# Attention scores by pairs of heads, a PSUM bank for each head, a list prefill in 22 pieces, and idle products in the front

## What is computed

```python
def attn(xn, in_proj_weight, out_proj_weight):        # xn [16, 256, 128]
    q, k, v = split_heads(xn @ in_proj_weight.T)      # 16 heads of 8
    attention = q @ k.T / sqrt(8) + causal_mask
    x = softmax(attention) @ v
    return x @ out_proj_weight.T

def ffn(xn, ...):                                     # inner width 352
    out = expert(xn, sg, su, sd)                      # the shared expert
    w = top2_of_softmax(xn @ wr.T + rb)               # 7 routed experts
    for e in range(7):
        out = out + w[..., e:e + 1] * expert(xn, rg[e], ru[e], rd[e])
    return out

x = x + attn(xn, ...) + ffn(xn, ...)
```

## Time and profile before

| | us |
|---|---|
| median of 3 runs | 547.07 |
| range of the runs | 542.17 to 549.5 |
| the profiled execution | 548.51 |
| its span | 546.8 |
| mean granted TensorE clock | 0.92 of full speed |

### The profile page before, as it was taken

The page is one execution under the profiler, slowest core; times in us unless marked ns, Lnnn a source line. Parts: engine busy times, 40 slices in busy tenths (PEclk is TensorE's granted clock), DMA queues, the critical chain, the costliest instruction groups (busy, mean ns, idle before and its releaser), DMA issues.

```text
span 546.8 us, 11856 instructions
## 1 busy us (share of the span) xinstructions
PE 487.8 (89%) x3924; PEld 355.8 (65%) x3924; DVE 388.4 (71%) x916; ACT 305.5 (56%) x543; POOL 309.8 (57%) x402
## 2 busy tenths in 40 slices
PE   2689987788899898898888779999999999999996
PEld 2667654455566565555555448888888888888884
DVE  5683688589978786777776227777777777776885
ACT  2434444446556566565555536666666666566654
POOL 1324466467763778788788700555555555584462
PEclk9875579779979999999999659999999999999999
DMA  8461478997765545554534253766666666502262
GB/s 259 144 187 48 112 288 306 366 309 248 253 207 184 157 143 150 162 164 151 167 102 152 63 218 107 247 225 233 216 227 213 238 233 241 201 17 79 91 202 93
DMA packets 53308, 101.18 MB, mean 185 GB/s; under 512 B 10295, under 2 KB 27584, under 8 KB 49280
## 3 DMA queue, kind: packets, MB, share of 16 engines
q1 hardware_dynamic: 48384, 91.95, 51.1%
q0 software_dynamic: 4864, 8.48, 4.7%
HBM read 60.91 MB, written 41.05 MB: 186 GB/s over the span
## 4 chain that ended last, share of the span: by engine, by line
PE 59%; issue 3%; ACT 2%; DVE 2%; POOL 1%; DVEq 0%; POOLq 0%; ACTq 0%
PE ps L624 12%; PE ps L625 12%; PE ps L626 11%; PE ps L754 4%; PE ps L684 3%; PE ps L678 2%; PE ps L863 2%; PE ps L764 2%; PE ps L690 2%; PE ps L852 2%; PE ps L744 2%; PE ps L757 1%; PE ps L700 1%; PE ps L766 1%; ACT sb_work L519 1%
## 5 line engine op out<-in xcount | busy, mean ns | idle before, releaser
L478 POOL DMA_INDIRECT ys<-sb_v_all,sb_xn_all x88 | 88.2, 1002 | 91.1 <-DVE sb_v_all L1135 66.4
L519 ACT ACTIVATE sb_work<-ps 128x1536 f32<-128x1536 f32 x64 | 92.9, 1452 | 45.2 <-PE ps L684 45.2
L443 POOL TENSOR_SCALAR_AFFINE_SELECT sb_work<-sb_work 128x768 f32<-128x768 f32 (+1 forms) x128 | 78.5, 639 | 65.4 <-DVE sb_mexp L1031 11.6
L1016 DVE TENSOR_REDUCE sb_negm<-ps 128x4 f32<-128x1024 f32 x64 | 78.3, 1223 | 46.5 <-PE ps L696 43.7
L624 PE MATMUL ps<-sb_ring,sb_wb 128*128 128x512 f32 x222 | 92.2, 415 | 2.3 <-DVE sb_ring L1109 1.6
L625 PE MATMUL ps<-sb_ring,sb_wb 128*128 128x512 f32 x222 | 88.7, 400 | 0.0
L626 PE MATMUL ps<-sb_ring,sb_wb 128*128 128x512 f32 x222 | 88.0, 396 | 0.0
L1123 DVE TENSOR_TENSOR sb_ring<-sb_work,sb_ring 128x512 fp32r<-128x512 f32 x90 | 64.4, 716 | 27.6 <-ACT sb_ring L587 21.8
L587 ACT ACTIVATE sb_ring<-sb_work 128x512 fp32r<-128x512 f32 x90 | 56.9, 632 | 46.2 <-DVE sb_work L1117 38.3
L1117 DVE TENSOR_TENSOR sb_work<-ps,sb_work 128x512 f32<-128x512 f32 x90 | 62.0, 689 | 24.7 <-ACT sb_work L581 16.4
L581 ACT ACTIVATE sb_work<-ps 128x512 f32<-128x512 f32 x90 | 53.7, 596 | 34.8 <-PE ps L626 26.2
(11 more groups left out here) (150 smaller groups left out, 1011.0 us busy)
## 6 DMA issues: line engine op xcount, KB each, us to landing
sb_wb<-wd SPq DMA_DIRECT2D x23, 1152.0 KB
sb_ring<-qk SPq DMA_DIRECT2D x64, 256.0 KB
wd<-sb_wb SPq DMA_DIRECT2D x8, 1152.0 KB, 6.1
sb_xn_all<-xs SPq DMA_DIRECT2D x22, 260.0 KB
qk<-sb_qk_h SPq DMA_DIRECT2D x16, 256.0 KB
qk<-sb_qk_l SPq DMA_DIRECT2D x32, 128.0 KB
qk<-sb_qk_h SPq DMA_DIRECT2D x32, 128.0 KB
sb_v_all<-ys SPq DMA_DIRECT2D x16, 256.0 KB, 3.1
```

What stands on the lines that cost most here:

```text
L443: pool.affine_select(out=o, in_=o, compare_op=ALU.is_ge, fill=0.0, base=0, pattern=[[0, o.shape[1]], [1, 128]], channel_multiplier=-1)\
L478: pool.indirect_dma_start(out=ys_d, out_offset=bass.IndirectOffsetOnAxis(ap=row, axis=0), in_=yst[i % NYS][:, EMB * j:EMB * j + EMB], in_o ...
L519: act.activation(P[n % 2], TR, ACT.Exp, scale=SCALE).then_inc(s["ex"], 1)
L1016: dve.tensor_reduce(negm[:, 1, :], SR[:, 256:1280].rearrange("p (h k) -> p h k", h=4), AX.X, ALU.max, negate=True).then_inc(s["maxa"], 1)
```

## The change

S and T get a bank for each head: S of head h in bank h, T of heads 0 and 2 in bank 4 and of 1 and 3 in bank 5, 384 columns each. The heads are served as two pairs. `scores(n, half)` forms S of one pair and T of the other, so each group of eight products meets four banks. Behind the first half come the transposes of quad n - 2 and the sums of quad n - 1, then the second half, then a wait for the normalization, the side products and the fold. `R1` is gone. The maxima come in two halves of two reductions each; between them stands the normalization, behind them the low part, `mexp` (now three buffers) and the routing piece. The exponential and the select come in two halves too, and the select waits for its exponential alone. The semaphore counts follow. The first two folds move from the front to its end. The prefill goes out in 22 pieces, one in each of the steps -1 to 20. TensorE gets 40 products of 512 columns whose result nobody reads: 22 at the start, 8 before the first v projection, 2 in each of the first five rounds of the front. In the front VectorE normalizes the first four token tiles ahead of the split of the small weights, and side results of steps below -4 go to banks 0 to 3.

```diff
-S0_AT, S1_AT = (0, 128, 1280, 1408), (256, 512, 768, 1024)
-T0_AT, T1_AT = (0, 512, 768, 1024), (256, 384, 1408, 1280)
+HEAD = 384
+PAIRS = ((0, 1), (2, 3))
...
+        S = [ps[:, h, 0:HEAD] for h in range(4)]
+        T = [ps[:, 4 + h % 2, 0:HEAD] for h in range(4)]
...
-            return J[:, 256:512] if n < -4 and n % 4 == 1 else X[:, 256:512]
+            return ps[:, n % 4, 256:512] if n < -4 else X[:, 256:512]
...
-                if n in (3, 5, 7, 9):
-                    if n == 3:
+                if 0 <= n + 1 < NR:
+                    if n == -1:
                         sp.wait_ge(s["ones1"], 1)
-                    a, z = [NR * k // 4 for k in ((n - 3) // 2, (n - 1) // 2)]
-                    sp.dma_start(xs_d.rearrange("(p a r) e -> p a (r e)", p=128, r=SUB)[:, a:z, :],
-                                 ones.unsqueeze(1).to_broadcast([128, z - a, SUB * ROW])).then_inc(s_zero, 16)
+                    rows = xs_d[TS * (n + 1):TS * (n + 2), :].rearrange("(p j) e -> p (j e)", j=SUB)
+                    sp.dma_start(rows, ones).then_inc(s_zero, 16)
...
-                    if isq(n + 3):
-                        pool.wait_ge(s["mx"], n + 4)
-                    if n < len(ROUTING):
-                        pool.wait_ge(s["rt"], sum(ROUTING[:n + 1]))
-                    pool.wait_ge(s["ex"], n + 1)
-                    for o in (parts[:, 0:12:2, :], parts[:, 3:12:8, :]):
+                    for k, pair in enumerate(PAIRS[::-1]):
+                        pool.wait_ge(s["ex"], 2 * n + k + 1)
+                        o = P[n % 2][:, HEAD * pair[0]:HEAD * pair[0] + 512].rearrange("p (k q) -> p k q", q=128)
                         pool.affine_select(out=o, in_=o, compare_op=ALU.is_ge, fill=0.0, base=0,
...
-                    act.wait_ge(s["ST"], n + 1)
-                    act.activation(P[n % 2], TR, ACT.Exp, scale=SCALE).then_inc(s["ex"], 1)
+                    for k, pair in enumerate(PAIRS[::-1]):
+                        act.wait_ge(s["ST"], 2 * n + k + 1)
+                        part = P[n % 2][:, HEAD * pair[0]:HEAD * pair[0] + 2 * HEAD]
+                        act.activation(part.rearrange("p (k h q) -> p h k q", h=2, q=128),
+                                       ps[:, 4:6, 0:HEAD].rearrange("p h (k q) -> p h k q", q=128), ACT.Exp,
+                                       scale=SCALE).then_inc(s["ex"], 1)
...
+            def scores(n, half):
                 m = n + 3
+                (a, b), (c, d) = PAIRS[half], PAIRS[1 - half]
                 if isq(m):
                     pe.wait_ge(s_qk[m % NK], m // NK * 16 + 16)
                     if m:
-                        pe.wait_ge(s["maxa"], m)
-                        pe.wait_ge(s["maxb"], m)
+                        pe.wait_ge(s["max"], 2 * m - 1 + half)
                 if isq(n):
                     pe.wait_ge(s["q4b"], n + 1)
-                    if n:
-                        pe.wait_ge(s["ex"], n)
+                    if n or half:
+                        pe.wait_ge(s["ex"], 2 * n + half)
...
-                pe.wait_ge(s["R1"], n + 4)
...
             def step(n):
                 b, j = quad(n)
                 if isq(n) or isq(n + 3):
-                    scores(n)
-                if n > -4:
-                    bank_read(n - 1)
-                side(n)
+                    scores(n, 0)
                 if isq(n - 2):
+                    bank_read(n - 1)
                     pe.wait_ge(s["OT"], n - 1)
                     for t in range(2):
                         last = pe.transpose(X[:, 128 * t:128 * t + 128], ot[:, 128 * t:128 * t + 128], ident)
                     last.then_inc(s["T"], 1)
                 if isq(n - 1):
+                    sums(n - 1)
+                if isq(n) or isq(n + 3):
+                    scores(n, 1)
+                if n > -4:
+                    bank_read(n - 1)
+                if isq(n - 2):
+                    pe.wait_ge(s["nm"], n - 1)
+                side(n)
+                if n >= 0 and isq(n + 2):
+                    maxima(n + 2)
...
+            def idle(count):
+                for _ in range(count):
+                    pe.matmul(X[:, :], busy[:, 0:128], busy[:, :], start=True, stop=True, skip_group_check=True)
+            pe.wait_ge(s["busy"], 1)
+            idle(22)
...
+                def maximum(half):
+                    a, b = PAIRS[half]
+                    dve.wait_ge(s["S"], 2 * m + half + 1)
+                    if half == 0 and m:
+                        dve.wait_ge(s["mx"], m)
+                    dve.tensor_reduce(negm[:, 1, a:b + 1], ps[:, a:b + 1, 0:256], AX.X, ALU.max, negate=True)
+                    dve.tensor_reduce(negm[:, 0, a:b + 1], ps[:, a:b + 1, 256:HEAD], AX.X, ALU.max, negate=True)\
+                        .then_inc(s["max"], 1)
```

233 lines of the change are left out of this document (109 added, 124 removed).

## The result

The changed kernel takes 546.9 us (median of 20 runs, 543.1 to 551.6), the kernel before 543.8 beside it (20 runs, 540.4 to 549.5). The ratio is 1.0056, with a 95% interval of 1.0029 to 1.0083: slower by half a per cent, where the prediction had it 0.7% faster. The profiled execution of the changed kernel took 551.6 us (span 549.9), in a slow state that 2 of its 20 runs show; that of before took 548.5.

The account below looks back on a forecast made before the run. Bound before: a ring of scores, all maxima, scores again, with GpSimd and VectorE close behind. Steps 5 to 22 -2, five routing steps +1, 32 late steps -3.5, rest 0: total -4, 542.3 to 543 us; range 525 to 560.

Parts of the forecast that it names:

- the one on GpSimd's waits: GpSimd's selects, freed from waits, may collide with VectorE's mexp and routing operations: 0.1 us a step, bounds 0 and 0.45.
- the slow rival: Collisions on VectorE cost 0.45 us per routing step (+8), four more low-clock spells +8: 559 us; chance 0.23.
- The rule that was weighed: GpSimd and VectorE share one port pair; by the rule, routing products collide as the cast does, giving the slow rival's time.
- the neutral case: Whole kernel: gain and loss cancel, likeliest at chance 0.42, its own range 536 to 552 us.
- VectorE and the normalization: TensorE waits for the normalization, late by VectorE's list of 3.65 us: routing steps 4.0 us, 0.25 slower than 3.76.
- GpSimd late: Steps 27 to 61: GpSimd's work with sends is a floor of 3.57 us a step; 3.65 taken, against 3.76 before.
- The ring: Old attention step: scores, all maxima, scores again; step = offset of the second score group + 2.6 us.
- ScalarE: One exponential becomes two of 0.81 us, +0.17 a step, hidden; 0.3 us lost in one step of four.
- Prefill: 22 small pieces instead of four remove the long q and k load stall: 3 us of DMA stalls left of 6.4.
- Idle products: 40 unread TensorE products cost some time and might keep the clock high: 0 taken for the sum.
- Low clock: After stalls, two spells at 1.2 GHz of about 2 us each; one should go with its stall.
- no edit there: Front, steps 0 to 4, tail and experts: change of 0 us in the sum.

Follow-up runs that it names:

- the extra one: One more VectorE reduction of 512 columns in each of steps 28 to 59: ratio 1.048 added to the changed kernel, 0.995 added to the kernel before.
- the last kernel: Changed kernel with GpSimd's split of the expert weights waiting for the step's mexp and routing in steps 0 to 22 only: 536.8 us, ratio 0.9917.

## Why the prediction was wrong

**The step that failed** is the one on GpSimd's waits: "The old waits kept selects away from VectorE's mexp and routing operations [...] Lower bound nothing, upper 0.45 a step; I take 0.1." The size is 0.4: VectorE's 0.55 more a step less 0.13 for the fourth reduction. It lies near the upper end, past the 0.3 from which the slow rival was said to decide. And the partner was wrong. The prediction named what stands behind the select (copy, split, sends), but used the list for GpSimd's load only. It did not ask what else the removed wait had been ordering: the split of 1.0 us, whose product reads two SBUF tiles. The cast of 0.62 us that it took as its measure had been held by just this instruction. The run without selects (VectorE still busy 72.6 us in steps 5 to 22) and those with the split delayed (68.3, and step 23 begins 9 to 15 us earlier) show it from two sides, and the kernel before with its selects freed shows that the removed wait alone brings the collisions (76.0).

**The rule that was weighed.** The trace shows a product with two SBUF inputs held until the split's product ends, and reductions of SBUF data untouched (the extra one took 0.68 us in both kernels, beside sends and selects; the routing's 0.54 and 0.55). The Trainium skill (SBUF — State Buffer, Who interferes with whom) says that VectorE instructions with two SBUF inputs contend with a GpSimd instruction that reads SBUF, that reductions do not on this chip, and that the shared port pair is an exclusive lock; the trace agrees on all three. The prediction took the rule as a rival and gave it less than the neutral case, although it saw itself that the old trace had uncontended products only where the selects were made to wait. They were uncontended because of the wait that the change removes, so they were no evidence against it, and the slow rival should have had the larger chance.

**VectorE and the normalization.** Reductions of 0.69 and 0.415 us as forecast (0.68, 0.41), and TensorE waits where it was said to. Forecast 4.0 us for routing steps; measured 4.69 in steps 5 to 22 (4.6 to 4.85 in the other traces). In steps 23 to 27, which have routing and no split, the 4.23 is this execution's, and the others have 3.84. With the split's collisions out (the last kernel) it is 4.13 and 3.83: the list itself was sized to 0.2 on either side.

**GpSimd late.** Forecast 3.65 against a floor of 3.57; measured 3.62, and 3.31 without sends, the 3.3 of TensorE alone. Right.

**The ring.** "Step = offset of the second group + 2.6" held for the two steps of the earlier trace rows, but its 3.76 was not the ring's alone: 3.55 without sends. The term was 0.2 too large, and would have misled had GpSimd not set the new step anyway.

**ScalarE.** 0.81 us forecast, 0.814 measured (128 exponentials). TensorE waits 1.7 us for it at the score products of L683 in the whole run, where 0.3 in every fourth step would be 5.

**Prefill.** One stall was forecast to go; all went. Alone it is worth 1.6% of the kernel before, 5 us or more. In the changed kernel it shows nothing, as steps held up by VectorE leave the loads time.

**Idle products.** Forecast 0, measured 0.

**Low clock.** One spell was forecast to go with its stall; the mean stayed (0.87, 0.88).

**The whole.** The terms of the sum give 542.3 us, and the span of the trace is 549.9: +6.2 in steps 5 to 27, +4.0 behind step 59, +0.6 ahead of the loop, -2.4 in steps 0 to 4 and -0.8 in the late steps. The 4.0 lies in steps 60 to 63. It was put at 0 under the words "no edit there", but these steps are edited too, and what they wait for was not studied. So the mechanism in steps 5 to 22 was the slow rival's, with little more than a third of its 16 us and without its four more spells of low clock. That the time came as near the forecast as it did is partly luck: the gain in steps 0 to 4 was not forecast.

## What to carry to other kernels

Before a wait is taken away, write down every instruction behind it in that engine's queue and what each would now run beside; a wait for one hazard may be what keeps the next instruction out of a collision. Time each part of a change on the old kernel alone, stage by stage: here one part was worth 1.6%, another cost 1.8% in a stage that the whole change leaves unharmed, and the whole looked like nothing. Before a step time is blamed on a change, see how far it moves between executions of the same code. When an early stage is made faster, look at the interval of every later stage before judging it.

## What was not expected of the hardware

GpSimd's sends did not hold up a VectorE product here, its selects did. In steps 28 to 59 of the changed kernel the two mexp operations take 0.385 and 0.348 us as a mean, without sends 0.194 and 0.184, which looks like the sends' doing. Sorted by what ran beside them, the product keeps 0.176 us in all 10 steps where it meets only a send (and in all 20 of the kernel before), and takes 0.53 where it meets a select. With sends in GpSimd's queue its selects come later, and 13 products meet one; without sends none does. Four casts in the two traces, which started 0.53 to 0.68 us into a send, were held until it was over (0.26 to 0.41 us). None of this sets the late step, as far as the traces show.

Signals of TensorE can come late while GpSimd sends. In the kernel before they come 0.7 us after the sums' last product in the late steps as a mean, up to 1.8, in the kernels with late steps of 4.4 to 4.5 us 0.84 to 0.95; in the changed kernel and in all without sends 0.04. VectorE's own signals, for the maxima and mexp, come 0.01 us after as a median. In 17 of 32 late steps of the kernel before the signal comes some 1.3 to 1.4 us after a send has started, just when the next one can (a send is 0.97 us long, the next follows 1.28 behind it). Why the changed kernel is spared, with as many sends, stays open, and so does what decides between 3.62 and 4.49 at its entry: it was seen that the same code from step 28 on can run either way, and that, among the kernels in the changed order with spread sends (the one with the selects' waits in all steps left out), step 28 takes about 4.5 us or more in those that stay at 3.6 to 3.7, while of the five others four have 3.56 to 4.04 there and one (with the extra operation) 4.49. No run here takes this apart further.
